# Cross-attention and routed experts on one core: x turned first in its slot, its statistics, its split and the placing of choices in other slots, a new order at the beginning

## The chip, the cores and the metric

One core of a Trainium2 chip runs the whole program. The metric is the device time of one execution in microseconds (us). The core has five engines that run in parallel, each through its own instructions in order: TensorE (PE; its weight loads are PEld), VectorE (DVE), ScalarE (ACT), GpSimd (POOL) and SyncE (SP), which here only issues transfers. They wait for one another by semaphores.

## The reference

For 64 sequences of 128 tokens with 512 features: layer norm, cross-attention to a context of 128 tokens (16 query heads on 4 heads of keys and values, head size 128, queries and keys RMS-normalised), a residual, a second layer norm, and a layer of 12 experts of which each token takes 2, with a limited number of places per expert.

```python
x = x + _L0_xattn_ref(_layernorm(x, axis=-1), ctx_2048, Wq, Wk, Wv, Wo, q_norm_w, k_norm_w)
x = x + _L0_ffn_ref(_layernorm(x, axis=-1), gate_w, w1, w2, w3)
# attention
q = rms_norm((hidden @ Wq), q_norm_w); k = rms_norm((enc @ Wk), k_norm_w); v = enc @ Wv
probs = softmax(q k^T / sqrt(128)); out = (probs @ v) @ Wo
# experts: top 2 of 12 by softmax(x @ gate_w.T), each expert takes its first cap tokens
```

## The kernel before

Two stages follow each other. The first, some 2180 us long, does attention, the second layer norm and the choice of experts; the second gathers each expert's tokens, computes and adds them. The change touches the first stage alone.

The first stage is a software pipeline. A block b is one sequence (64 of them); a slot (b, g) is one of its four steps, one for each head of keys, so g runs from 0 to 3. On each engine a function `body(b)` goes through the four slots and does in each the work of several blocks at different depths: `body` runs for b = -1 to 66, with b = 3 to 60 as a loop on the chip. What stands in `body` under `if g == ...` sets by hand the order in which each engine does things; nothing is reordered later. Semaphores only make an engine wait.

Every number is multiplied as a pair of float16: a high part, rounded on ScalarE (`split_...` of ScalarE), and the rest, formed on VectorE (`split_...` of VectorE, helpers at L1058 and L1063). A matmul takes three products of parts. Left operands must lie turned, which SyncE does by transfers (`turn_...`, L635): q, p (probabilities), k, c (context), x, xn2 (the second norm).

What the main functions are, in the order of a slot (u = 4b + g):
- TensorE: scores of u (L788), keys or values of block b+1 (L744, wkv), queries of u+3 (L744, wq; they need the turned x of block b+1 from slot (b, 1) on), the output product of u-2 (L813), attention of u-1 (L801).
- VectorE: `maxima` of the scores (L1123, L1126), low half of the outputs (L1063), other splits, `normalise` (reciprocal L1132, product L1135), low half of the probabilities (L1058, p), low half of the queries (L1114), and then one or two jobs at the end of the slot.
- ScalarE: `exps` (L943), high halves of the probabilities (L951) and queries (L933), squares of the queries (L924).
- GpSimd: roots and scales on 128 numbers or 128 x 4, and the scatter of choices to the token table (`scatter`, L1487).

The path of x, block b+2 seen from body b: loaded in slot 0 (`load_x`, L619), statistics `stats_x` (L1078, L1082) at the end of slot 0 on VectorE, reciprocal deviation `rstd_of_x` on GpSimd in slot 1, `norm_x` (L1086) at the end of slot 1, high half on ScalarE in slot 3 (L897), low half on VectorE (`split_x`, L1058) in slot 0 of body b+1, then the turn in the same slot. Choices: `choose` in slot 1 of body b+2, `count` in slot 2, `place` (L1205 to L1231) in slot 3, `scatter` in slot 0 of body b+3. `place` writes into the entries that `scatter` sends.

Before all that, the weights are scaled by their root mean square and split too. A lot is one quarter of Wq or Wo, or all of Wk or Wv (1 MB each). For each: `sum_of_lot` (squares, L1266 on VectorE or L972 on ScalarE), a total over partitions on TensorE (L736) that VectorE copies (`copy_lot_total`, L1273), the scale on GpSimd, `head_of_lot` (L979) on ScalarE and `rest_of_lot` (L1280) on VectorE. These stand between the work of the first blocks.

## Time and profile before

| | |
|---|---|
| median of 3 runs | 2544.46 us (2543.19 to 2546.59) |
| profiled execution | 2528.24 us, its span 2526.5 us |
| TensorE busy | 2277.3 us (90%) |
| VectorE busy | 1871.3 us (74%) |
| ScalarE busy | 1748.6 us (69%) |
| GpSimd busy | 1080.2 us (43%) |
| DMA moved | 348.03 MB, mean 138 GB/s |

How to read it: the busy shares are means over the run; the second stage, after some 2180 us, is less busy on all engines but GpSimd. The granted clock of TensorE is full in nearly all of the first stage. A row of a group or of a timeline gives the line, the engine, the operation, written<-read tiles, shapes and count; `[0.75 <-ACT ...]` behind it is the idle time ahead of it and what ended that. Times in a timeline are from the start of the span. Tiles are named as in the program; `work` holds probs, x_res, raw_c, raw_x and kn, and `small` all small vectors.

### The profile page before, as it was taken

Reading aid. Unit: us, or ns where it says so; the run is one execution under the profiler, and the core shown is the slowest. Engines: PE = TensorE matmul, PEld = TensorE weight load, DVE = VectorE, ACT = ScalarE, POOL = GpSimd, SP = SyncE. Lnnn points to the kernel's source line nnn. Section 1 sums busy time; section 2 is a strip of 40 time slices with the busy share of each in tenths; the row PEclk is TensorE's granted clock in tenths of the full one; section 3 lists DMA queues with packets and bytes.
Section 4 is the critical chain, followed back from the end, with each engine's and each line's share of the span. In section 5 each row is a group of like instructions: output and inputs, shape, how many; then the busy total and the mean of one; then the engine's idle time right before and its main releaser. Section 6 shows DMA issues by size and latency. Waiting matters only on the chain. (4 is left out here: it accounts for less than half of the span.)

```text
span 2526.5 us, 54978 instructions
## 1 busy us (share of the span) xinstructions
PE 2277.3 (90%) x12931; PEld 1143.1 (45%) x12931; DVE 1871.3 (74%) x5158; ACT 1748.6 (69%) x6911; POOL 1080.2 (43%) x1949
## 2 busy tenths in 40 slices
PE   3899999999999999999999999999999999659883
PEld 1444444444444444444444444444444444335541
DVE  6777777777777877777777778777777787536552
ACT  6877777777777777777767777777777777435441
POOL 6333333343343333343333333333343333268885
PEclk8999999999999999999999999999999999879775
DMA  8576666666666666666666666666666666459997
GB/s 249 101 140 131 137 133 133 130 132 133 137 131 135 141 129 132 133 133 133 133 125 141 134 136 134 134 131 135 131 138 131 137 141 130 88 151 189 174 176 96
DMA packets 894359, 348.03 MB, mean 138 GB/s; under 512 B 829004, under 2 KB 829260, under 8 KB 894288
## 3 DMA queue, kind: packets, MB, share of 16 engines
q1 hardware_dynamic: 869104, 300.20, 56.8%
q0 software_dynamic: 22912, 43.16, 9.6%
q10 hardware_dynamic: 2304, 4.24, 0.5%
q8 instruction: 14, 0.23, 0.0%
q14 instruction: 25, 0.20, 0.0%
HBM read 91.37 MB, written 57.71 MB: 59 GB/s over the span
## 5 line engine op out<-in xcount | busy, mean ns | idle before, releaser
L744 PE MATMUL pb<-wq,xT 128*128 128x512 f16 x3072 | 718.8, 384 | 93.9 <-DMA xT<-x 92.6
L943 ACT ACTIVATE work<-pb,small 128x128 f32<-128x128 f32 x1024 | 455.2, 453 | 395.2 <-DVE small L1126 395.2
L813 PE MATMUL pb<-wo,o 128*128 128x512 f16 x3072 | 711.6, 381 | 13.3 <-DVE o L1063 13.0
L1393 POOL TENSOR_TENSOR small<-small 128x4 f32<-128x4 f32 (+1 forms) x584 | 494.7, 850 | 59.8 <-POOL small L1464 18.4
L744 PEld LDWEIGHTS pb<-wq,xT 128*128 128x128 f16 x3072 | 298.5, 99 | 480.6 <-issue 137.6
L813 PEld LDWEIGHTS pb<-wo,o 128*128 128x128 f16 x3072 | 286.8, 98 | 346.4 <-DVE o L1063 17.8
L744 PE MATMUL pb<-wkv,cT 128*128 128x512 f16 x1536 | 376.6, 381 | 4.7 <-DVE wq L1280 4.7
L1464 POOL TENSOR_TENSOR small<-small 128x4 f32<-128x4 f32 x256 | 55.3, 216 | 751.7 <-ACT junk_q L924 747.2
L1114 DVE SCALAR_TENSOR_TENSOR q<-pb,small,q 128x128 f16<-128x128 f32 x1024 | 288.3, 344 | 70.4 <-ACT q L933 70.4
L933 ACT ACTIVATE q<-pb,small 128x128 f16<-128x128 f32 x1024 | 291.1, 366 | 2.6 <-POOL small L1393 1.8
L1058 DVE TENSOR_TENSOR p<-work,p 128x512 f16<-128x512 f32 x256 | 177.3, 692 | 142.9 <-ACT p L951 137.1
L924 ACT ACTIVATE junk_q<-pb 128x128 bf16<-128x128 f32 x1024 | 273.4, 305 | 5.2 <-PE pb L744 5.2
L924 ACT ACTIVATION_READ_ACCUMULATOR junk_q<-pb 128x1 f32 x1024 | 243.9, 238 | 0.0
L788 PEld LDWEIGHTS pb<-kT,qT 128*128 128x128 f16 x3072 | 193.1, 98 | 70.1 <-issue 10.2
L788 PE MATMUL pb<-kT,qT 128*128 128x128 f16 x3072 | 213.9, 219 | 8.8 <-DMA kT<-k 8.0
L951 ACT CAST p<-work 128x512 f16<-128x512 f32 x256 | 158.2, 618 | 86.0 <-DVE work L1135 85.2
L801 PE MATMUL pb<-pT,v 128*128 128x512 f16 x768 | 208.1, 380 | 0.0
L943 ACT ACTIVATION_READ_ACCUMULATOR work<-pb,small 128x1 f32 x1024 | 202.7, 198 | 0.0
L1123 DVE TENSOR_REDUCE small<-pb 128x4 f32<-128x512 f32 x256 | 176.3, 689 | 29.8 <-issue 23.1
L744 PEld LDWEIGHTS pb<-wkv,cT 128*128 128x128 f16 x1536 | 140.2, 98 | 127.8 <-DVE wq L1280 4.8
L1487 POOL DMA_INDIRECT token_table<-small x128 | 152.3, 1189 | 85.2 <-issue 68.2
L1135 DVE SCALAR_TENSOR_TENSOR work<-work,small 128x512 f32<-128x512 f32 x256 | 177.2, 692 | 8.8
(146 smaller groups left out, 2913.6 us busy)
## 6 DMA issues: line engine op xcount, KB each, us to landing
work<-x SPq DMA_DIRECT2D x128, 256.0 KB, 3.1
work<-c SPq DMA_DIRECT2D x64, 256.0 KB, 2.8
out<-work SPq DMA_DIRECT2D x64, 256.0 KB, 2.0
xn_scratch<-work SPq DMA_DIRECT2D x64, 256.0 KB, 2.1
wq_raw<-wq SPq DMA_DIRECT2D x4, 1024.0 KB, 13.3
wo_raw<-wo ACTq DMA_DIRECT2D x4, 1024.0 KB, 11.5
qT<-q SPq DMA_TRANSPOSE x256, 3.1
pT<-p SPq DMA_TRANSPOSE x256, 3.2
```

The source lines that it names most:

```text
L744: mm = nc.tensor.matmul(bank[:, :], lhs[:, NC * a + c, :], rhs[b_][:, c, :], start=(c == 0 and n == 0), stop=(c == NC - 1 and n == 2))
L788: mm = nc.tensor.matmul(S_B[:, h * 128:(h + 1) * 128], qT16[g % 2][:, 4 * a + h, :], kT16[:, 4 * b_ + g, :], start=(n == 0), stop=(n == 2))
L801: mm = nc.tensor.matmul(OT_B[:, :], v16[:, NG * a + g, :], pT16[g % 2][:, (HI, LO)[b_], :], start=(n == 0), stop=(n == 2))
L813: mm = nc.tensor.matmul(WO_B[:, :], o16[:, HPG * a + h, :], part(O0 + g, b_)[:, h, :], start=(g == 0 and h == 0 and n == 0), stop=(g == NG ...
L924: sq = nc.scalar.activation(junk_q[:, h, :], Q_BS[g % 2][:, h * 128:(h + 1) * 128], ACT.Square, scale=1.0 / QS, accum_out=q_ssq[:, h:h + 1])
L933: hi = nc.scalar.activation(q16[:, h, :], Q_BS[g % 2][:, h * 128:(h + 1) * 128], ACT.Copy, scale=q_rms[g % 2][:, h:h + 1])
L943: ex = nc.scalar.activation(probs[:, cols], S_B[:, cols], ACT.Exp, bias=nmax[:, h:h + 1], scale=esc, accum_out=psums[:, h:h + 1])
L1058: return nc.vector.tensor_tensor(pair[:, LO, :], whole.rearrange(by_head, h=4), pair[:, HI, :], ALU.subtract)
L1114: lo = nc.vector.scalar_tensor_tensor(out=q16[:, 4 + h, :], in0=Q_BS[g % 2][:, h * 128:(h + 1) * 128], scalar=q_rms[g % 2][:, h:h + 1], in ...
L1123: nc.vector.tensor_reduce(smax, heads(S_B), AX.X, ALU.max).then_inc(mx_done, 1)
L1135: nc.vector.scalar_tensor_tensor(out=pv, in0=pv, scalar=PS, in1=rsums[:, :, None].broadcast_to([128, HPG, 128]), op0=ALU.mult, op1=ALU.mul ...
L1393: return nc.gpsimd.tensor_tensor(out_, in_, neghalf[:, 0:n], ALU.pow)
```

## The change

Steady part, on each engine:
- SyncE: in slot 0, `load_x` and `turn_x` come ahead of `turn_xn2`.
- VectorE: `split_x` leaves slot 0 of the next body and becomes the last work of slot 3; `stats_x` goes from the end of slot 0 to the end of slot 1; `norm_x` from the end of slot 1 to the front of slot 3, ahead of `split_k`; `place` from the end of slot 3 to the end of the next slot 0.
- GpSimd: `scatter` from slot 0 to slot 1, `rstd_of_x` from slot 1 to slot 2.

Beginning: Wq's lots 1 to 3 are loaded by ScalarE's queue instead of SyncE's; the turn of c and the load and turn of x are issued earlier, the second c, the gate and the fill of the tables later; the sums of Wo's lots come after the work of block 0 in their slot, the loads of Wo at the end of slot (-1, 1); further sums, totals and rests change places.

```diff
@@ sync
-                for g in range(1, NG):
-                    load_lot(Q0 + g)
...
+                turn_c(0)
...
-                turn_c(0)
-                load_c(1)
-                sp.wait_ge(s_const, 1)
-                fill_tables()
...
-                        if g == 0 and live(b - 2):
-                            turn_xn2(b - 2)
                         if g == 0 and live(b + 2):
                             load_x(b + 2)
                         if g == 0 and live(b + 1):
                             turn_x(b + 1)
+                        if g == 0 and live(b - 2):
+                            turn_xn2(b - 2)
+                        if g == 0 and isinstance(b, int) and b == -1:
+                            load_c(1)
+                            sp.dma_start(gate[:, :, :], gateT).then_inc(d_gate, 16)
+                            sp.wait_ge(s_const, 1)
+                            fill_tables()
@@ scalar
                 sum_c(0)
+                load_lot(act, Q0 + 1)
                 sum_of_lot(K0)
                 split_c(0)
+                load_lot(act, Q0 + 2)
                 split_x(0)
+                load_lot(act, Q0 + 3)
                 sum_of_lot(V0)
...
-                            if g == 1:
-                                for l in ALL_O:
-                                    load_wo(l)
-                            if g == 3:
-                                sum_of_lot(O0 + 2)
-                                sum_of_lot(O0 + 3)
...
+                        if isinstance(b, int) and b == -1 and g == 1:
+                            for l in ALL_O:
+                                load_wo(l)
+                        if isinstance(b, int) and b == -1 and g == 3:
+                            sum_of_lot(O0 + 2)
+                            sum_of_lot(O0 + 3)
@@ vector
-                        if g == 0 and live(b + 1) and not (isinstance(b, int) and b == -1):
-                            split_x(b + 1)
...
+                        if g == 3 and live(b + 2):
+                            norm_x(b + 2)
                         if g == 3 and live(b + 1):
                             split_k(b + 1)
...
-                        if g == 0 and live(b + 2):
-                            stats_x(b + 2)
+                        if g == 0 and live(b - 3):
+                            place(b - 3)
                         if g == 1 and live(b - 2):
                             choose(b - 2)
                         if g == 1 and live(b + 2):
-                            norm_x(b + 2)
+                            stats_x(b + 2)
...
-                        if g == 3 and live(b - 2):
-                            place(b - 2)
+                        if g == 3 and live(b + 2):
+                            split_x(b + 2)
+                        if isinstance(b, int) and b == -1 and g == 3:
+                            sum_of_lot(O0)
+                            sum_of_lot(O0 + 1)
@@ gpsimd
-                        if g == 0 and live(b - 3):
+                        if g == 1 and live(b - 3):
                             scatter(b - 3)
-                        if g == 1 and live(b + 2):
-                            rstd_of_x(b + 2)
...
+                        if g == 2 and live(b + 2):
+                            rstd_of_x(b + 2)
```

SyncE at the start of body 2 (slot 0). Before:
```order
L635 DMA_TRANSPOSE qT_1<-q 128x8x128
L635 DMA_TRANSPOSE nT<-n 128x8x128
L619 DMA work<-x 128x512
L635 DMA_TRANSPOSE xT<-x 128x8x128
L635 DMA_TRANSPOSE pT_0<-p 128x8x128
```
The change, with its own line numbers (nine more here):
```order
L644 DMA_TRANSPOSE qT_1<-q 128x8x128
L628 DMA work<-x 128x512
L644 DMA_TRANSPOSE xT<-x 128x8x128
L644 DMA_TRANSPOSE nT<-n 128x8x128
L644 DMA_TRANSPOSE pT_0<-p 128x8x128
```
The turn of xn2 (nT) has gone behind the load and the turn of x.

VectorE from the maxima of slot (2, 3) to the end of that slot, just ahead of the loop. Before:
```order
L1123 TENSOR_REDUCE small<-pb 128x4
L1126 TENSOR_SCALAR small<-small 128x4
L1063 SCALAR_TENSOR_TENSOR o<-pb,o 128x512
L1058 TENSOR_TENSOR k<-work,k 128x512
L1132 RECIPROCAL small<-small 128x4
L1135 SCALAR_TENSOR_TENSOR work<-work,small 128x512
L1058 TENSOR_TENSOR p<-work,p 128x512
L1114 SCALAR_TENSOR_TENSOR q<-pb,small,q 128x128 x4
L1165 TENSOR_SCALAR work<-work,small 128x512
L1205 TENSOR_SCALAR small<-small 128x1
L1207 TENSOR_REDUCE small<-small 128x2
```
The change (two more in the line numbers of VectorE):
```order
L1125 TENSOR_REDUCE small<-pb 128x4
L1128 TENSOR_SCALAR small<-small 128x4
L1065 SCALAR_TENSOR_TENSOR o<-pb,o 128x512
L1088 TENSOR_SCALAR work<-work,small 128x512
L1060 TENSOR_TENSOR k<-work,k 128x512
L1134 RECIPROCAL small<-small 128x4
L1137 SCALAR_TENSOR_TENSOR work<-work,small 128x512
L1060 TENSOR_TENSOR p<-work,p 128x512
L1116 SCALAR_TENSOR_TENSOR q<-pb,small,q 128x128 x4
L1167 TENSOR_SCALAR work<-work,small 128x512
L1060 TENSOR_TENSOR x<-work,x 128x512
```
norm_x (L1086, now L1088) has come in ahead of the low half of k, and the low half of x stands where `place` began (L1205 onward, 11 operations).

VectorE from the end of slot (-1, 3) to the first maxima. Before:
```order
L1280 SCALAR_TENSOR_TENSOR wq<-wq_raw,small,wq 128x512 x4
L1266 SCALAR_TENSOR_TENSOR wo,small<-wo_raw 128x2048 x2
L1058 TENSOR_TENSOR k<-work,k 128x512
L1114 SCALAR_TENSOR_TENSOR q<-pb,small,q 128x128 x4
L1123 TENSOR_REDUCE small<-pb 128x4
```
The change:
```order
L1088 TENSOR_SCALAR work<-work,small 128x512
L1060 TENSOR_TENSOR k<-work,k 128x512
L1282 SCALAR_TENSOR_TENSOR wq<-wq_raw,small,wq 128x512 x4
L1116 SCALAR_TENSOR_TENSOR q<-pb,small,q 128x128 x4
L1060 TENSOR_TENSOR x<-work,x 128x512
L1268 SCALAR_TENSOR_TENSOR wo,small<-wo_raw 128x2048 x2
L1125 TENSOR_REDUCE small<-pb 128x4
```
The two squared sums of Wo have gone from ahead of the low half of k to behind everything else of the slot. TensorE's order is the same in both.

## Rows read from the trace of the kernel before

**Rows 1.** The page: busy time of each engine, and the query matmuls' group.
```profile
PE 2277.3 (90%) x12931; PEld 1143.1 (45%) x12931; DVE 1871.3 (74%) x5158; ACT 1748.6 (69%) x6911; POOL 1080.2 (43%) x1949
...
L744 PE MATMUL pb<-wq,xT 128*128 128x512 f16 x3072 | 718.8, 384 | 93.9 <-DMA xT<-x 92.6
```

**Rows 2.** Timeline of TensorE: the scores that open one block and the next.
```profile
999.27 0.83 PE L788 MATMUL pb<-kT,qT 128*128 128x128 f16 x12
...
1030.88 0.83 PE L788 MATMUL pb<-kT,qT 128*128 128x128 f16 x12
```

**Rows 3.** The line of the row maxima, 200 to 2140 us: count, durations, first and last.
```profile
L1123 DVE TENSOR_REDUCE small<-pb x233: 677/691/693, 203.6 to 2136.1; 128x4 f32<-128x512 f32 x117
```

**Rows 4.** Waits of VectorE, 200 to 2140 us: us in total, times, longest.
```profile
DVE small L1078 <- DMA work<-x: 47.2, 54, 3.1
...
DVE small L1123 <- PE pb L788: 2.1, 7, 0.3
```

**Rows 5.** Timeline of VectorE over one block, slots 1, 2, 3, 0.
```profile
1009.29 0.69 DVE L1123 TENSOR_REDUCE small<-pb 128x4 f32<-128x512 f32 x1
...
1016.89 0.54 DVE L1086 TENSOR_SCALAR work<-work,small 128x512 f32<-128x512 f32 x1
1017.35 0.74 DVE L1151 SCALAR_TENSOR_TENSOR work<-pb,small,work 128x512 f32<-128x512 f32 x1
...
1025.44 0.69 DVE L1123 TENSOR_REDUCE small<-pb 128x4 f32<-128x512 f32 x1
...
1028.33 0.18 DVE L1132 RECIPROCAL small<-small 128x4 f32<-128x4 f32 x1 [0.75 <-ACT work L943]
...
1032.46 0.15 DVE L1205 TENSOR_SCALAR small<-small 128x1 f32<-128x1 f32 x1
...
1034.09 0.69 DVE L1123 TENSOR_REDUCE small<-pb 128x4 f32<-128x512 f32 x1 [0.40 <-issue]
...
1036.15 0.68 DVE L1058 TENSOR_TENSOR x<-work,x 128x512 f16<-128x512 f32 x1
1036.98 0.18 DVE L1132 RECIPROCAL small<-small 128x4 f32<-128x4 f32 x1
...
1040.87 0.69 DVE L1078 BATCH_NORM_STATS2 small<-work 128x6 f32<-128x512 f32 x1
...
1041.84 0.69 DVE L1123 TENSOR_REDUCE small<-pb 128x4 f32<-128x512 f32 x1
```

**Rows 6.** Waits of all engines, whole run.
```profile
DVE small L1078 <- DMA work<-x: 55.9, 58, 6.6
```

**Rows 7.** Timeline of the same block: SyncE's queue and ScalarE.
```profile
1027.65 1.23 SPq L635 DMA_TRANSPOSE kT<-k  x1
...
1036.40 0.46 ACT L943 ACTIVATE work<-pb,small 128x128 f32<-128x128 f32 x1
...
1038.44 1.24 SPq L635 DMA_TRANSPOSE xT<-x  x1
```

**Rows 8.** Landing times: of k's turn over the run, of x's by its tile.
```profile
kT<-k SPq DMA_TRANSPOSE x64, 3.1
...
DMA to landing us min/median/max: 3.6/4.1/6.7
```

**Rows 9.** Timeline of VectorE in the beginning; the page's row on the loads of Wo.
```profile
26.48 0.16 DVE L1273 TENSOR_SCALAR small<-pb 128x1 f32<-128x1 f32 x1 [2.93 <-PE pb L736]
...
41.74 0.16 DVE L1273 TENSOR_SCALAR small<-pb 128x1 f32<-128x1 f32 x1 [3.21 <-PE pb L736]
...
51.39 2.29 DVE L1266 SCALAR_TENSOR_TENSOR wo<-wo_raw 128x2048 f16<-128x2048 f32 x1
...
55.77 1.12 DVE L1114 SCALAR_TENSOR_TENSOR q<-pb,small,q 128x128 f16<-128x128 f32 x4 [1.47 <-ACT q L933]
59.02 0.69 DVE L1123 TENSOR_REDUCE small<-pb 128x4 f32<-128x512 f32 x1 [2.13 <-PE pb L788]
...
wo_raw<-wo ACTq DMA_DIRECT2D x4, 1024.0 KB, 11.5
```

More of the change, by code:

```diff
@@ L608, in loop, with load_lot @@
                     body(b)
+            wkv_v = [w.rearrange("(c p) n -> p c n", p=128) for w in (wk, wv)]
+            wq_v = wq.rearrange("(c p) n -> p c n", p=128)
+            def load_lot(eng, l):
+                kind, n = LOTS[l]
+                src = wq_v[:, :, n * 512:(n + 1) * 512] if kind == "q" else wkv_v["kv".index(kind)]
+                eng.dma_start(raw(l), src).then_inc(d_w[l], 16)
             @block.sync
@@ L661, in turn_xn2 @@
                     turn(nT16, n16, d_nT)
-                wkv_v = [w.rearrange("(c p) n -> p c n", p=128) for w in (wk, wv)]
-                wq_v = wq.rearrange("(c p) n -> p c n", p=128)
-                def load_lot(l):
-                    kind, n = LOTS[l]
-                    src = wq_v[:, :, n * 512:(n + 1) * 512] if kind == "q" else wkv_v["kv".index(kind)]
-                    sp.dma_start(raw(l), src).then_inc(d_w[l], 16)
                 def fill_tables():
@@ L679, in _ @@
                 load_c(0)
[L680 removed]
+                load_lot(sp, K0)
                 load_x(0)
[L682 to L685 removed]
+                load_lot(sp, Q0)
+                load_lot(sp, V0)
+                turn_c(0)
                 sp.dma_start(wb[:, :], qw.broadcast_to([128, HD])).then_inc(d_small, 16)
                 sp.dma_start(wk_row[:, :], kw.broadcast_to([128, HD])).then_inc(d_small, 16)
[L688 to L692 removed]
                 def body(b):
@@ L1003, in body @@
                         last = off(b, g, -2)
-                        for l in at_slot(HEADS, b, g):
-                            head_of_lot(l)
-                        if isinstance(b, int) and b == -1:
-                            if g == 0:
-                                sum_of_lot(Q0 + 3)
-                            if g == 1:
-                                for l in ALL_O:
-                                    load_wo(l)
-                            if g == 3:
-                                sum_of_lot(O0 + 2)
-                                sum_of_lot(O0 + 3)
                         if live(last[0]):
@@ L1024, in body @@
                             split_k(b + 1)
+                        for l in at_slot(HEADS, b, g):
+                            head_of_lot(l)
+                        if isinstance(b, int) and b == -1 and g == 0:
+                            sum_of_lot(Q0 + 3)
                         if live(b):
@@ L1291, in _ @@
                 copy_total(0)
+                split_x(0)
                 sum_of_lot(Q0)
-                split_x(0)
                 copy_lot_total(Q0)
@@ L1296, in _ @@
                 copy_lot_total(V0)
+                rest_of_lot(Q0)
                 sum_of_lot(Q0 + 1)
-                rest_of_lot(Q0)
                 def body(b):
@@ L1303, in body @@
                         last = off(b, g, -2)
-                        if isinstance(b, int) and b == -1:
-                            if g == 0:
-                                copy_lot_total(Q0 + 1)
-                                sum_of_lot(Q0 + 2)
-                                rest_of_lot(V0)
-                            if g == 1:
-                                copy_lot_total(Q0 + 2)
-                                rest_of_lot(Q0 + 1)
-                                scale_weights()
-                            if g == 2:
-                                copy_lot_total(Q0 + 3)
-                                rest_of_lot(Q0 + 2)
-                            if g == 3:
-                                rest_of_lot(Q0 + 3)
-                                sum_of_lot(O0)
-                                sum_of_lot(O0 + 1)
                         if g == 0 and isinstance(b, int) and b == 1:
@@ L1335, in body @@
                             norm_k(b + 1)
+                        if g == 3 and live(b + 2):
+                            norm_x(b + 2)
                         if g == 3 and live(b + 1):
                             split_k(b + 1)
+                        if isinstance(b, int) and b == -1:
+                            if g == 0:
+                                copy_lot_total(Q0 + 1)
+                                rest_of_lot(V0)
+                                sum_of_lot(Q0 + 2)
+                            if g == 1:
+                                copy_lot_total(Q0 + 2)
+                                scale_weights()
+                                rest_of_lot(Q0 + 1)
+                            if g == 2:
+                                copy_lot_total(Q0 + 3)
+                                rest_of_lot(Q0 + 2)
+                            if g == 3:
+                                rest_of_lot(Q0 + 3)
                         if live(b):
```

4 lines of the change are left out of this document (removed).

## The prediction

> **What bounds the kernel now.** I read the page first, then the waits of each engine in a long steady stretch (200 to 2140 us), then one block instruction by instruction, and last the first 60 us.
>
> The page points at TensorE: 90% busy, VectorE 74%, and one large named stall, the query matmuls (L744) held 92.6 us by the transfer that turns x [rows 1]. If that were the bound, the change would be worth those 92.6 us. So the question is who holds whom. A block in which TensorE is hardly held takes it 1030.88 - 999.27 = 31.6 us from its first scores to the next block's [rows 2]. The row maxima on VectorE (L1123) come four times a block; over the stretch their 233 starts are (2136.1 - 203.6) / 232 = 8.33 us apart, 33.3 us a block [rows 3]. TensorE is thus ahead by 1.7 us a block and has to stop somewhere. VectorE, in the same stretch, is held by TensorE for 2.1 us in all at the maxima, and by nothing else of TensorE; it stops 47.2 us for x to arrive, 0.40 us a block at the turn of its loop [rows 4, 5], and otherwise for ScalarE's halves of the same work (exp, probabilities, queries), which ScalarE in its turn can begin only when VectorE hands them over. VectorE and ScalarE form a closed chain and set the pace. TensorE's stall on x is where its spare time shows, not what it costs.
>
> The chain in one block [rows 5]: from maxima to maxima slots 1 and 2 take 1025.44 - 1009.29 = 16.15 us, slot 3 8.65, slot 0 1041.84 - 1034.09 = 7.75, together 32.55. In this block x was not waited for; with its mean wait of 47.2 / 58 = 0.81 us the block is 33.36, against the 33.3 measured. So this account of the block is complete, and the change has to be priced on it.
>
> **The change, part by part, for the chain.**
>
> *Statistics of x out of slot 0.* stats_x comes one slot later, so x has a slot, some 8 us, more to arrive. VectorE no longer waits: 55.9 us over the run, of which the first, 6.6 us, is the very first x and stays [rows 6]. That is -49.3 us. The operation itself, 1041.84 - 1040.87 = 0.97 us, is at the open end of a slot before and after and costs the same there.
>
> *Normalising x from slot 1 to slot 3.* At the end of slot 1 nothing covers it: it takes 1017.35 - 1016.89 = 0.46 us until the next operation starts. Its new place is ahead of the reciprocal in slot 3, where VectorE idles 0.75 us for the exponentials [rows 5]. It fits with 0.29 to spare: -0.46 x 62 blocks = -28.5 us. The two first blocks are part of the beginning.
>
> *Low half of x (split_x, L1058) from slot 0 to the end of slot 3.* This one goes the wrong way. In slot 0 it stands ahead of the reciprocal and ends at 1036.83, while the last exponential, which the reciprocal needs too, ends at 1036.40 + 0.46 = 1036.86 [rows 5, 7]. It was free there and taking it away gains nothing. At the end of slot 3 nothing covers its 0.68 us: +42 us over 62 blocks (0.60 each if it overlaps its neighbours as VectorE's operations do in the middle of a slot, +37).
>
> *Choices placed (place) from slot 3 to slot 0.* Its 11 small operations take from 1032.46 until the 0.40 idle before 1034.09, 1.23 us [rows 5], uncovered before and after: 0. The scatter that follows them moves to slot 1 on GpSimd, ahead of the mean squares of k. Those are needed by VectorE only in slot 2; that cover gone, each us that they were late would cost one per block.
>
> *Turn of x first.* split_x now precedes the slot, so load and turn of x can be issued as soon as SyncE has sent the queries, and are not behind the turn of xn2. In the block shown the turn was issued at 1038.44 [rows 7]; before it stood the turn of xn2, which waited for VectorE's slot 0. I expect it about 2.5 us earlier, enough for its 4.1 us to land [rows 8] ahead of the queries in nearly all blocks. The stall at L744 goes away; but TensorE will stop elsewhere, since it still is quicker than the chain: I expect at the turned k (scores, L788) and for the low half of queries and outputs. Worth by itself: 0.
>
> *The turn of k.* normalising x also stands ahead of split_k, so k's turn is issued 0.46 us later. It was issued at 1027.65 [rows 7], and lands in 3.1 us [rows 8]: with 0.46 more, 1031.21, scores done 0.83 later [rows 2], 1032.04, some 0.1 for the hand-over. The maxima of that slot would start at 1034.09 - (1.23 - 0.68) = 1033.54. So 1.4 us of slack cover this; VectorE doesn't wait.
>
> Sum for the blocks: -49.3 - 28.5 + 42.2 = -35.6 us, 0.57 a block; new pace about 32.7 us, still above TensorE's 31.6.
>
> **The beginning.** The first maxima stand at 59.02. Ahead of them VectorE idled 2.13 us for the scores and 1.47 for a slice of queries; the scores waited for k, whose low half stood behind two squared sums of Wo at 2.29 us [rows 9]. The change puts k ahead of these sums: both waits, 3.60 us, should go. Two earlier waits, 2.93 and 3.21 us for totals of weights [rows 9], hang on the second c and on the first queries, whose transfers come earlier now that three weight slices go by ScalarE's queue; I count 2 of the 6.1. Against it split_x of block 1 is done earlier, +0.7. Together -5. The bounds: -9 if all four waits go; 0 if the loads of Wo, now issued after the first squared queries and 11.5 us on the way [rows 9], come late for the sums that then stand last, or if the two queues of weights delay the v weights, on which ScalarE waits ahead of its first split.
>
> The end has no x, and its chain of choices runs in the same order: 0.
>
> **Sum.** -35.6 - 5 = -40.6 us. The profiled execution took 2528.24 us around its span of 2526.5, 16 us less than the median of the runs, 2544.46; it should come out at 2487.6. The difference carried to the median: 2503.9, say 2504.
>
> **A rule to weigh.** The Trainium skill (Perfetto Trace Analysis, Identifying Performance Opportunities) says to optimise the engine with the highest occupancy first and to look for what ends its gaps. It warns that TensorE's busy share is no good measure of its distance from the roofline, yet by the rule as it stands TensorE is the one to relieve, and its gap is the wait for x. By it this change would be worth the whole stall, which is the first rival below. The rows on who waits for whom contradict it here.
>
> **Rivals.**
> *The stall is the cost.* If relieving TensorE let the chain follow, the 92.6 us would go, with 5 at the beginning: 2447. For it: the stall is real and comes in every block. Against it: VectorE's 2.1 us of waiting for TensorE; there is almost nothing for an earlier TensorE to speed up, unless ScalarE's waits hide some.
> *The cover in slot 3 fails.* ScalarE's split of x stands in slot 3 right behind the exponentials and ahead of the probabilities. If the normalised x comes late there, the 28.5 us aren't gained: -49.3 + 42.2 - 5 = -12, 2532. The 0.29 to spare says no, narrowly.
> *Slower: k's turn.* If it took 5.5 us instead of 3.1 once it shares the queue in another rhythm, VectorE would wait 2.4 - 1.4 = 1.0 a block: +62 - 41 = +21, 2565. It decides from about 3.1 + 1.4 + 0.66 = 5.2 us on. x's turn, the same size, needs 4.1 in the median and up to 6.7 [rows 8], so it isn't absurd; in the long stretch the scores aren't held today.
> *No change.* The reciprocal root of x on GpSimd, moved to slot 2 ahead of its other work, could come late for slot 3 and give back most of what the wait for x cost: with 0.65 us a block of it, +40 - 41, 2544. Against it: a whole slot lies between, and GpSimd is 43% busy [rows 1].
>
> **How the numbers follow.** My forecast (2490 to 2518: uncovered split_x at 0.60 or 0.69 us, the beginning -9 to 0, runs scattering by 3 us) 0.64. The full stall 0.08. Cover fails or a like partial loss 0.14. No change 0.05. Slower 0.09. Faster by more than 0.2% (5 us, about what a measurement of this kernel can tell from no change) is 0.64 + 0.08 + 0.14 = 0.86, the same 0.05, slower 0.09. The range from 2476 to 2532 leaves out the full stall, the slower case and part of no change.
>
> **What would show it.** The maxima's spacing falls from 8.33 us to about 8.18, slots 1 and 2 together from 16.15 to 16.7, slot 3 from 8.65 to 8.1, slot 0 from 8.56 (with its wait) to 8.0. The waits for x on VectorE and at L744 are gone to the first; TensorE has new waits of over 1 us a block at the scores or for low halves, and is still busy as long as before. Wrong would be: VectorE's maxima waiting for scores (then k or TensorE bounds), the reciprocal in slot 3 later than before, or maxima spaced below 8.0.

## The result

The changed kernel takes 2481.03 us (median of 4 runs, 2479.44 to 2482.33); the kernel before, on the same chip, 2543.82 us (4 runs, 2538.54 to 2546.59). The ratio is 0.9755, 95% interval 0.9738 to 0.9772: 62.8 us less. The profiled executions took 2528.24 us before and 2481.03 us after (span 2479.3), 47.2 us less. The forecast was 2504, range 2476 to 2532.

The page of the changed kernel, its busy row and three groups. These answer to [rows 1] and to the line of the maxima, now L1125:
```profile
PE 2279.2 (92%) x12931; PEld 1143.6 (46%) x12931; DVE 1877.1 (76%) x5158; ACT 1749.1 (71%) x6911; POOL 1055.1 (43%) x1949
...
L744 PE MATMUL pb<-wq,xT 128*128 128x512 f16 x3072 | 709.0, 381 | 2.1 <-DMA xT<-x 1.2
...
L788 PE MATMUL pb<-kT,qT 128*128 128x128 f16 x3072 | 214.7, 220 | 37.9 <-DMA kT<-k 36.1
...
L1125 DVE TENSOR_REDUCE small<-pb 128x4 f32<-128x512 f32 x256 | 175.7, 686 | 2.6 <-issue 0.3
```
TensorE is busy as long as before; its stall on x, 92.6 us, is 1.2 us. It stops for k instead.

Waits of VectorE in the changed kernel, 200 to 2140 us (answers to [rows 4]), complete:
```profile
DVE p L1060 <- ACT p L951: 128.8, 182, 0.8
DVE small L1134 <- ACT work L943: 89.2, 188, 1.3
DVE q L1116 <- ACT q L933: 64.5, 238, 0.8
DVE small L1134 <- issue: 35.7, 52, 0.7
```
x is waited for no more, TensorE not either: the chain of VectorE and ScalarE is still closed.

One block on VectorE in the changed kernel, slots 1, 2, 3 and the start of the next (answers to [rows 5]):
```profile
1016.66 0.16 DVE L1233 TENSOR_TENSOR small<-small 128x2 int32<-128x2 f32 x1
1016.83 0.69 DVE L1125 TENSOR_REDUCE small<-pb 128x4 f32<-128x512 f32 x1
...
1024.52 0.69 DVE L1080 BATCH_NORM_STATS2 small<-work 128x6 f32<-128x512 f32 x1
...
1026.16 0.68 DVE L1125 TENSOR_REDUCE small<-pb 128x4 f32<-128x512 f32 x1
...
1033.74 0.69 DVE L1125 TENSOR_REDUCE small<-pb 128x4 f32<-128x512 f32 x1
...
1035.21 0.54 DVE L1088 TENSOR_SCALAR work<-work,small 128x512 f32<-128x512 f32 x1
...
1036.64 0.18 DVE L1134 RECIPROCAL small<-small 128x4 f32<-128x4 f32 x1 [0.29 <-ACT work L943]
...
1040.76 0.69 DVE L1060 TENSOR_TENSOR x<-work,x 128x512 f16<-128x512 f32 x1
1041.37 0.68 DVE L1125 TENSOR_REDUCE small<-pb 128x4 f32<-128x512 f32 x1
```
The normalising of x (L1088) stands in the gap ahead of slot 3's reciprocal and leaves 0.29 of its 0.75 us. The low half of x (L1060) stands uncovered at the slot's end, 0.61 us. The maxima behind it begin at once: the 0.40 us of idle time at the loop's turn [rows 5] is gone, which was not foreseen. The last of the eleven operations of the placing (L1233) now stands directly ahead of the maxima of slot 1, with no turn of the loop between them, and no idle time is seen there.

The beginning on VectorE in the changed kernel (answers to [rows 9]):
```profile
56.76 1.13 DVE L1116 SCALAR_TENSOR_TENSOR q<-pb,small,q 128x128 f16<-128x128 f32 x4 [5.36 <-ACT q L933]
...
58.40 2.28 DVE L1268 SCALAR_TENSOR_TENSOR wo<-wo_raw 128x2048 f16<-128x2048 f32 x1
...
60.61 2.29 DVE L1268 SCALAR_TENSOR_TENSOR wo<-wo_raw 128x2048 f16<-128x2048 f32 x1
...
62.82 0.69 DVE L1125 TENSOR_REDUCE small<-pb 128x4 f32<-128x512 f32 x1
```
The wait for queries is 5.36 us instead of 1.47, and both squared sums of Wo now stand between it and the first maxima. The scores that these maxima read, on TensorE, in the kernel before:
```profile
57.54 1.44 PE L788 MATMUL pb<-kT,qT 128*128 128x128 f16 x12 [8.02 <-DMA kT<-k]
```
And in the changed kernel:
```profile
57.42 1.44 PE L788 MATMUL pb<-kT,qT 128*128 128x128 f16 x12 [6.90 <-DMA kT<-k]
```
The scores end as early as before, 57.42 + 1.44 = 58.86 instead of 58.98. The maxima follow them at once before (59.02), and 3.96 us later in the changed kernel (62.82), when VectorE has done the sums.

Where the 47.2 us of the profiled executions lie: first maxima at 62.82 instead of 59.02, +3.8; from the first to the last of the 256 maxima 2067.7 instead of 2124.2, -56.5; behind them 348.8 instead of 343.3, +5.5.

### The profile page after: what moved, and what is told of

It reads as the page before. It is cut to its first block and busy times, and to the rows that moved or that the text cites. A ratio compares the mean times of both kernels' runs of the same rounds, so it can differ in the third digit from the quotient of the medians.

```text
span 2479.3 us, 54980 instructions
## 1 busy us (share of the span) xinstructions
PE 2279.2 (92%) x12931; PEld 1143.6 (46%) x12931; DVE 1877.1 (76%) x5158; ACT 1749.1 (71%) x6911; POOL 1055.1 (43%) x1949
## 5 line engine op out<-in xcount | busy, mean ns | idle before, releaser
L744 PE MATMUL pb<-wq,xT 128*128 128x512 f16 x3072 | 709.0, 381 | 2.1 <-DMA xT<-x 1.2
L1396 POOL TENSOR_TENSOR small<-small 128x4 f32<-128x4 f32 (+1 forms) x584 | 484.1, 833 | 60.9 <-POOL small L1467 18.4
L744 PEld LDWEIGHTS pb<-wq,xT 128*128 128x128 f16 x3072 | 300.8, 98 | 367.3 <-DVE q L1116 13.6
L744 PE MATMUL pb<-wkv,cT 128*128 128x512 f16 x1536 | 377.1, 382 | 2.9 <-DVE wkv L1282 2.9
L1060 DVE TENSOR_TENSOR p<-work,p 128x512 f16<-128x512 f32 x256 | 177.3, 692 | 142.9 <-ACT p L951 137.1
L788 PE MATMUL pb<-kT,qT 128*128 128x128 f16 x3072 | 214.7, 220 | 37.9 <-DMA kT<-k 36.1
L744 PEld LDWEIGHTS pb<-wkv,cT 128*128 128x128 f16 x1536 | 140.3, 98 | 126.1 <-issue 3.3
L1125 DVE TENSOR_REDUCE small<-pb 128x4 f32<-128x512 f32 x256 | 175.7, 686 | 2.6 <-issue 0.3
L1065 DVE SCALAR_TENSOR_TENSOR o<-pb,o 128x512 f16<-128x512 f32 x256 | 175.0, 683 | 2.6 <-ACT o L957 2.5
```

What stands on the lines that cost most here:

```text
L744: mm = nc.tensor.matmul(bank[:, :], lhs[:, NC * a + c, :], rhs[b_][:, c, :], start=(c == 0 and n == 0), stop=(c == NC - 1 and n == 2))
L788: mm = nc.tensor.matmul(S_B[:, h * 128:(h + 1) * 128], qT16[g % 2][:, 4 * a + h, :], kT16[:, 4 * b_ + g, :], start=(n == 0), stop=(n == 2))
L1060: return nc.vector.tensor_tensor(pair[:, LO, :], whole.rearrange(by_head, h=4), pair[:, HI, :], ALU.subtract)
L1125: nc.vector.tensor_reduce(smax, heads(S_B), AX.X, ALU.max).then_inc(mx_done, 1)
L1396: return nc.gpsimd.tensor_tensor(out_, in_, neghalf[:, 0:n], ALU.pow)
```

## What each kernel's slots take

From the starts of the maxima on VectorE, mean of the 51 blocks between the 25th and the 229th of them, in us. Times are medians; "before" is the kernel before on the chip of the same runs. The slots of each kernel are from its one trace, that of "before" too. The runs below went in three sets, each on one chip: e1 to e4, f0 to f3, f4 to f7.

| kernel | slot 0 | slot 1 | slot 2 | slot 3 | block | time | before | ratio, 95% |
|---|---|---|---|---|---|---|---|---|
| before | 8.54 | 8.73 | 7.48 | 8.65 | 33.41 | | | |
| changed | 7.87 | 9.33 | 7.58 | 7.63 | 32.41 | 2481.0 | 2543.8 | 0.9755 (0.9738 to 0.9772) |
| e1_norm2_last | 9.31 | 8.76 | 7.53 | 8.29 | 33.89 | 2558.1 | 2524.4 | 1.0132 (1.0106 to 1.0158) |
| e2_stats_alone | 6.79 | 9.46 | 7.54 | 8.65 | 32.45 | 2475.2 | 2524.4 | 0.9804 (0.9779 to 0.9830) |
| e3_old_queue_order | 7.87 | 9.34 | 7.58 | 7.63 | 32.42 | 2474.5 | 2524.4 | 0.9797 (0.9772 to 0.9821) |
| e4_split_x_covered | 7.87 | 9.34 | 7.58 | 7.02 | 31.81 | 2439.3 | 2524.4 | 0.9661 (0.9637 to 0.9686) |
| f0_changed_again | 7.87 | 9.33 | 7.58 | 7.63 | 32.41 | 2480.3 | 2557.0 | 0.9700 (0.9683 to 0.9717) |
| f1_lots_late | 7.87 | 9.33 | 7.58 | 7.63 | 32.40 | 2482.8 | 2557.0 | 0.9707 (0.9691 to 0.9724) |
| f2_wo_early | 7.87 | 9.33 | 7.58 | 7.63 | 32.40 | 2478.4 | 2557.0 | 0.9697 (0.9681 to 0.9713) |
| f3_best | 7.87 | 9.33 | 7.57 | 7.02 | 31.79 | 2446.7 | 2557.0 | 0.9573 (0.9557 to 0.9589) |
| f4_place_alone | 8.84 | 8.73 | 7.43 | 7.02 | 32.01 | 2454.6 | 2543.6 | 0.9643 (0.9619 to 0.9667) |
| f5_place_last | 6.64 | 9.33 | 7.46 | 9.24 | 32.68 | 2498.3 | 2543.6 | 0.9816 (0.9793 to 0.9839) |
| f6_wo_early_covered | 7.86 | 9.33 | 7.57 | 7.02 | 31.78 | 2441.9 | 2543.6 | 0.9593 (0.9570 to 0.9616) |
| f7_gaps | 7.87 | 8.52 | 7.27 | 7.78 | 31.45 | 2420.7 | 2543.6 | 0.9510 (0.9482 to 0.9538) |

## The experiments on the blocks

**e1_norm2_last.** VectorE's slot 3 of the kernel before in another order: the placing no longer last.
```diff
-                        if g == 3 and live(b - 1):
-                            norm2(b - 1)
                         if g == 3 and live(b - 2):
                             place(b - 2)
+                        if g == 3 and live(b - 1):
+                            norm2(b - 1)
```


> The kernel before with one swap: in slot 3 VectorE places the choices first and then does the second norm (one operation of 0.54 us), so a long operation and not eleven short ones stands ahead of the turn of its loop. Theory A (the 0.40 us idle ahead of the maxima of slot 0 is time in which VectorE's instruction stream turns the loop, seen because the short operations don't cover it): the idle goes, slot 3 falls from 8.65 to about 8.25, 58 blocks, -23 us against before. Theory B (the idle is the price of the loop's turn whatever stands ahead): no change, and the 0.48 us by which slot 3 fell more than I priced came from elsewhere.

Measured: 2558.1 us, 34 slower than before. Both theories missed the time; slot 3 did as A said. It fell from 8.65 to 8.29 us, and the idle time at the loop's turn is gone. But slot 0 grew by 0.77. VectorE's wait for x, 200 to 2100 us:
```profile
DVE small L1078 <- DMA work<-x: 89.1, 57, 3.6
```
And one slot 0 in the timeline, with SyncE's queue:
```profile
1008.95 0.69 DVE L1123 TENSOR_REDUCE small<-pb 128x4 f32<-128x512 f32 x1
...
1011.47 1.23 SPq L635 DMA_TRANSPOSE nT<-n  x1
...
1012.95 0.41 SPq L619 DMA_DIRECT2D work<-x  x1
...
1016.76 0.69 DVE L1078 BATCH_NORM_STATS2 small<-work 128x6 f32<-128x512 f32 x1 [1.08 <-DMA work<-x]
```
The load is issued 4.00 us behind the slot's maxima; in the block of [rows 5] it was 3.69. The queue's own waits, 200 to 2100 us, say why:
```profile
SPq L434 <- DVE work L1165: 97.0, 56, 1.7
```
In the kernel before this wait is 32.8 us. It is that of the store of the second normalisation's result (L632, `store_xn2`), which stands in the queue ahead of the turn of queries, of the turn of xn2 (nT) and of the load of x. The low half of xn2 itself is not later: it starts 1.47 us behind the maxima in both kernels. The wait for x rose from 47.2 us [rows 4] to 89.1, 0.7 us a block; besides the 0.3 us of later issue, the load also took longer to land, 4.1 us in the median against 3.7. So that wait lies on a loop from VectorE over SyncE's queue back to VectorE, and a small delay of an operation that feeds the queue cost more than the order saved.

**e2_stats_alone.** The kernel before with the statistics of x in slot 1, the root in slot 2 and the normalising in slot 3; the low half of x and the placing stay where they were.
```diff
-                        if g == 0 and live(b + 2):
-                            stats_x(b + 2)
...
                         if g == 1 and live(b + 2):
-                            norm_x(b + 2)
+                            stats_x(b + 2)
...
+                        if g == 3 and live(b + 2):
+                            norm_x(b + 2)
```


> The kernel before with only the statistics of x moved to slot 1, its reciprocal deviation to slot 2 on GpSimd and its normalising to slot 3; the low half of x stays in slot 0, choices stay in slot 3, the queue's order and the beginning stay. Theory A (VectorE and ScalarE are a closed chain that sets the pace): the wait for x goes (-49) and the normalising is covered (-28), together about -75 us against before, more than the whole change gave, while TensorE still waits for the turned x in some blocks. Theory B (TensorE's wait for the turned x is the cost): the turned x comes no earlier in its slot, so little is won, 0 to -20 us.

Measured: -49 us, between the two, in the blocks -0.96 us. The wait for x is gone. What kept it from A's size shows in all engines' waits, 200 to 2100 us:
```profile
ACT o L957 <- PE pb L801: 117.2, 127, 2.3
...
PE pb L744 <- DMA xT<-x: 44.2, 48, 2.7
...
DVE small L1123 <- PE pb L788: 9.9, 41, 0.6
```
Here the chain is no longer closed: TensorE still waits 44.2 us for the turned x, ScalarE waits for TensorE's outputs (117.2 us, before 20.3), VectorE for its scores. That the turn of x stands where it was is not enough to explain it: in f4 and e3 it stands there too, and TensorE's wait for it is 1.4 and 0.8 us. What e2 has otherwise than these two is the write of the choices (`scatter`, GpSimd) still in slot 0, and a slot 0 shorter by 1 to 2 us; which of them counts, no run separates. The idle time at the loop's turn is as before, 22.3 us, since the placing still stands last.

**f4_place_alone.** The kernel before with the placing moved, and with it, of need, the write of the choices on GpSimd one slot later.
```diff
+                        if g == 0 and live(b - 3):
+                            place(b - 3)
                         if g == 0 and live(b + 2):
                             stats_x(b + 2)
...
-                        if g == 3 and live(b - 2):
-                            place(b - 2)
...
-                        if g == 0 and live(b - 3):
+                        if g == 1 and live(b - 3):
                             scatter(b - 3)
```


> The kernel before with one part of the change alone: the eleven small operations of the choices' placing go from the end of slot 3 to slot 0 ahead of the statistics of x (and the write of their table one slot later on GpSimd). Theory A (this part alone removes both the wait for x, 0.8 us a block, since it stands under it, and the 0.40 us in which VectorE stands at its loop's turn behind these operations): slot 3 falls from 8.65 to about 7.0 us, slot 0 rises from 8.5 to about 9.0, together -1.2 us a block, -75 us. Theory B (the idle time at the loop's turn has nothing to do with them): -0.8 us a block, -50 us. Theory C (x is late whatever stands ahead of it, because its load is due later too): -20 us or less.

Measured: 2454.6 against 2543.6, -89 us: more than the whole change gives. Theory A holds for the slots (7.02 and 8.84 for 7.0 and 9.0); its -75 us was 14 too little. Its timeline of all engines:
```profile
1024.86 0.68 DVE L1123 TENSOR_REDUCE small<-pb 128x4 f32<-128x512 f32 x1
...
1028.97 0.38 SPq L619 DMA_DIRECT2D work<-x  x1
...
1032.74 0.69 DVE L1078 BATCH_NORM_STATS2 small<-work 128x6 f32<-128x512 f32 x1
```
The load in the block of [rows 5], from the timeline of the kernel before:
```profile
1037.78 0.38 SPq L619 DMA_DIRECT2D work<-x  x1
```
There it is issued 3.69 us behind the slot's maxima, in f4 4.11, so no earlier. But the statistics are wanted 7.88 us behind the maxima instead of 1040.87 - 1034.09 = 6.78. The eleven small operations are a cover of 1.10 us, of which the later issue takes 0.42.

They are not the whole of it, since the load also lands sooner. The load of x from issue to landing, 200 to 2100 us, in the kernel before:
```profile
DMA to landing us min/median/max: 2.9/3.7/6.2
```
And in f4:
```profile
DMA to landing us min/median/max: 2.7/2.9/3.1
```
An estimate from these figures: with f4's landings even the kernel before would hardly wait, since its load would be there at the latest 3.69 + 3.1 = 6.79 us behind the maxima, for statistics wanted at 6.78. With the landings of before, f4 would still wait in some blocks: 4.11 + 6.2 = 10.3 at the most, for 7.88. What else moved in f4 is the write of the choices. In the kernel before it stands just ahead of the load (issued at 1037.78):
```profile
1034.97 1.12 POOL L1487 DMA_INDIRECT token_table<-small  x1 [0.76 <-issue]
...
1036.40 1.29 POOL L1487 DMA_INDIRECT token_table<-small  x1 [0.31 <-issue]
```
In all three kernels with this write in slot 0 (before, e1, e2) the load lands in 3.6 to 4.1 us in the median and up to 6.3; in those with it a slot later, in 2.9 us or less. So the write is a rival of the cover: f4 does not tell which of the two took the wait away, and no run moves the write by itself.

**f5_place_last.** The changed kernel with the placing at the end of slot 3 again, behind the low half of x.
```diff
-                        if g == 0 and live(b - 3):
-                            place(b - 3)
...
                         if g == 3 and live(b + 2):
                             split_x(b + 2)
+                        if g == 3 and live(b - 2):
+                            place(b - 2)
```


> The changed kernel with the placing last in slot 3 again, behind the split of x. Theory A (the loop's turn costs 0.40 us a block when eleven operations of 0.15 us stand ahead of it and nothing behind one of 0.5 us or more): slot 0 falls by 1.2 and slot 3 rises by 1.2 + 0.4 us, the period goes from 32.41 to 32.8 us, +26 us: 2506. Theory B (the idle went with something else, the load of the loop's own instructions for example): the period stays at 32.4 and the time at 2480.

Measured: 2498.3, where A had 2506 and B 2480; the block 32.68 instead of 32.8. A's mechanism came, its size in part. VectorE at its loop's turn:
```profile
1014.58 0.15 DVE L1231 TENSOR_SCALAR small<-small 128x1 f32<-128x1 f32 x1
1014.70 0.16 DVE L1233 TENSOR_TENSOR small<-small 128x2 int32<-128x2 f32 x1
1015.26 0.69 DVE L1125 TENSOR_REDUCE small<-pb 128x4 f32<-128x512 f32 x1 [0.40 <-issue]
```
And that wait, 200 to 2100 us:
```profile
DVE small L1125 <- issue: 22.3, 56, 0.4
```
The 0.40 us is back in every one of 56 blocks: slots 0 and 3 take 15.89 us instead of 7.87 + 7.63 = 15.50. The rest is slot 2, 0.12 shorter; why, no run tells.

**e4_split_x_covered.** The changed kernel with the low half of x back in slot 0, ahead of the reciprocal.
```diff
                         if g == 0 and live(b - 2):
                             split_xn2(b - 2)
+                        if g == 0 and live(b + 1) and not (isinstance(b, int) and b == -1):
+                            split_x(b + 1)
...
-                        if g == 3 and live(b + 2):
-                            split_x(b + 2)
```


> The changed kernel with the low half of x back in slot 0, ahead of the reciprocal, where VectorE idles 0.75 us for the exponentials in the changed kernel. Theory A (closed chain; this move was the change's loss): 0.60 us a block less, -37 us against the changed kernel, 2444; if the 0.40 us at the turn of the loop come back, since the operation that now stands last is the shorter second norm, 2467. Theory B (the turned x must come early): the turn goes behind slot 0's work again and TensorE is held by it, 2481 or slower.

Measured: 2439.3, and 35 us below e3 beside it; slot 3 fell by 0.61 and no other slot changed. So this move of the change cost what it was priced at, 0.60 us a block, and bought nothing. The idle time at the loop's turn does not return with the second normalisation (0.54 us) last.

**e3_old_queue_order.** The changed kernel with SyncE's turn of xn2 ahead of the load and the turn of x, as before.
```diff
+                        if g == 0 and live(b - 2):
+                            turn_xn2(b - 2)
                         if g == 0 and live(b + 2):
                             load_x(b + 2)
                         if g == 0 and live(b + 1):
                             turn_x(b + 1)
-                        if g == 0 and live(b - 2):
-                            turn_xn2(b - 2)
```


> The changed kernel with SyncE's old order alone: in slot 0 the turn of xn2 stands ahead of the load and the turn of x again. Theory A (closed chain on VectorE and ScalarE): the time of the changed kernel within 3 us, 2478 to 2484. Theory B (the early turn of x is what gains): x is turned some 1.5 us later and a part of the stall of before returns, 2500 or more.

Measured: 2474.5, below A's 2478 to 2484, and the same slots to 0.01 us. The turn of x first is worth nothing, as A said. TensorE's wait for the turned x, 200 to 2100 us:
```profile
PE pb L744 <- DMA xT<-x: 0.8, 2, 0.5
```
The stall of the kernel before (88.1 us in this stretch) stays away with the turn in its old place, issued 4.33 us behind the maxima in the mean, in before 4.35. So it was not the earlier turn that ended it.

## The experiments on the beginning

**f0_changed_again** is the changed kernel, unedited.

> The changed kernel unedited, on the chip of the runs beside it, as the level for them. Theory A (the time of before hangs on when x lands, that of the changed kernel does not): before moves with the chip, the changed kernel stays at 2474 to 2484 us. Theory B (chips differ alike for both): the ratio to before is 0.9755 again whatever the chip.

Measured: 2480.3, where before took 2557.0. The ratio is 0.9700 instead of 0.9755, their intervals apart, so theory B is out and A's numbers hold. Over four sets of runs before stood at 2524.4, 2543.6, 2543.8 and 2557.0; the changed kernel, in two of them, at 2481.0 and 2480.3, and e3, with the same slots, at 2474.5 beside the 2524.4. That it is the landing of x that makes before differ is argued; only one execution of it has a trace.

**f1_lots_late.** The changed kernel with ScalarE's loads of Wq behind its sum of v's weights.
```diff
                 sum_c(0)
-                load_lot(act, Q0 + 1)
...
                 sum_of_lot(V0)
+                load_lot(act, Q0 + 1)
+                load_lot(act, Q0 + 2)
+                load_lot(act, Q0 + 3)
```


> Beginning only: the changed kernel with ScalarE's three loads of lots of Wq (1, 2, 3) issued behind its sum of v's weights. Theory A (v's weights landed 4.2 us later, at 17.5 instead of 13.2 us, because the load of Wq's lot 1 runs beside theirs): the sum of v's weights starts at about 13.3 us, the first maxima at 59 to 60 instead of 62.8 us, and the time falls by 2 to 4 us. Theory B (something else holds the beginning, above all the landing of k and q turned for the first block): the sum is earlier and the first maxima stay at 62.5 to 63 us. The blocks stay at 32.41 us each.

Measured: 2482.8, not told from f0 by the time; the first maxima at 65.2 us, 2 later than in f0. The sum of v's weights did come early, as A said, and the Wq lots then came too late. The sum of v's weights on ScalarE, in the timeline of the kernel before:
```profile
13.23 1.91 ACT L972 ACTIVATE wkv<-wkv_raw 128x2048 f16<-128x2048 f32 x1 [2.34 <-DMA wkv_raw<-wv]
```
The same in the changed kernel:
```profile
17.47 1.91 ACT L972 ACTIVATE wkv<-wkv_raw 128x2048 f16<-128x2048 f32 x1 [6.43 <-DMA wkv_raw<-wv]
```
The same in f1, and VectorE's copy of a total there:
```profile
12.95 1.91 ACT L972 ACTIVATE wkv<-wkv_raw 128x2048 f16<-128x2048 f32 x1 [2.15 <-DMA wkv_raw<-wv]
...
32.27 0.16 DVE L1275 TENSOR_SCALAR small<-pb 128x1 f32<-128x1 f32 x1 [8.37 <-PE pb L736]
```
The sum came 4.5 us earlier, and the wait for the total of the next lot took 8.37 us, in the changed kernel 1.51.

**f2_wo_early.** The changed kernel with ScalarE's loads of Wo at the start of slot 1 of block -1.
```diff
+                        if isinstance(b, int) and b == -1 and g == 1:
+                            for l in ALL_O:
+                                load_wo(l)
                         if live(last[0]):
                             split_o(*last)
```


> Beginning only: the changed kernel with ScalarE's loads of Wo issued at the start of slot 1 of block -1 again, as before the change. Theory A (the turns of q and k before the first scores are late because 4 MB of Wo, issued at 39.9 to 42.2 us, run beside them): the loads are issued some 6 us earlier, the waits of 4.6 us for q's landing and 6.9 us for k's shrink by 4 to 5 us together with the first maxima, from 62.8 to about 58 us, and the time falls by 4 to 5 us. Theory B (the turns are late by their own chain: root and split of k): no change, first maxima at 62.5 to 63 us. The blocks stay at 32.41 us each.

Measured: 2478.4, the first maxima at 60.54 us against 63.26 in f0: -2.7. By the time alone that is not told from no change (interval of the ratio to before 0.9681 to 0.9713, f0's 0.9683 to 0.9717); the trace shows the mechanism. SyncE's queue in the changed kernel:
```profile
47.71 1.38 SPq L644 DMA_TRANSPOSE qT<-q  x1
49.20 4.37 SPq L644 DMA_TRANSPOSE cT<-c  x1
53.66 1.71 SPq L644 DMA_TRANSPOSE kT<-k  x1
```
And in f2:
```profile
48.99 1.27 SPq L644 DMA_TRANSPOSE cT<-c  x1
50.35 1.29 SPq L644 DMA_TRANSPOSE kT<-k  x1
```
In the changed kernel the turn of c holds the queue 4.37 us instead of 1.27, and k's turn goes 3.3 us later. Two of the four loads of Wo were then still under way (they landed at 51.27 and 54.83); in f2 all had landed by 46.49. A's size, 4 to 5 us, was too large by half.

## Versions made from the runs

**f3_best** is e4 with the edits of f1 and f2.

> A version made from what the runs showed: the changed kernel with the split of x back in slot 0 under the exponentials (which took 0.60 us a block off), ScalarE's Wq loads behind its sum of v's weights and its Wo loads early. Theory A (the blocks and the beginning add up): blocks of 31.81 us, 2430 to 2440 us. Theory B (the beginning is covered by something else, or a block falls into TensorE's floor of 31.5 us and waits return): 2439 us or more.

Measured: 2446.7, 33.6 below f0. The blocks are A's 31.79; the first maxima, at 62.75, gained almost nothing (f1's loss and f2's gain are about as large). Theory B's time.

**f6_wo_early_covered** is e4 with f2's edit alone.

> A version made from what the runs showed: the changed kernel with the split of x back in slot 0 under the exponentials, and ScalarE's Wo loads early; the Wq loads stay where the change put them. Theory A (both gains add up): first maxima at about 60 us, blocks of 31.80 us, 2435 to 2438 us. Theory B (a block of the covered version gains nothing from an earlier beginning): 2440 to 2447.

Measured: 2441.9. The first maxima (60.18) and the blocks (31.78) are A's, the time is B's: in its profiled execution what lies behind the last maxima took 353.0 us, against 339 to 349 in most others. That part was not looked into.

**f7_gaps** is f6 with three operations moved into the gap between the normalise and the split of P.
```diff
                         if g == 0 and live(b + 2):
                             split_c(b + 2)
+                        if g == 1 and live(b + 2):
+                            stats_x(b + 2)
+                        if g == 2 and live(b - 1):
+                            stats_2(b - 1)
+                        if g == 3 and live(b - 1):
+                            norm2(b - 1)
                         if live(b):
                             split_p(*cur)
...
-                        if g == 1 and live(b + 2):
-                            stats_x(b + 2)
-                        if g == 2 and live(b - 1):
-                            stats_2(b - 1)
-                        if g == 3 and live(b - 1):
-                            norm2(b - 1)
```


> The version beside it with three more operations under cover: the statistics of x in slot 1, those of the second normalisation in slot 2 and that normalisation in slot 3 stand between the normalise and the split of P, where VectorE waits 0.7 us for ScalarE. Theory A (the pace now passes to TensorE, which was busy 1880 of 1900 us in the covered version): blocks of 31.5 us, -20 us, 2416. Theory B (the chain through VectorE and ScalarE still sets it, and each operation delays the split of P by more than it saves): no gain or up to 20 us slower.

Measured: 2420.7, 21 below f6 and the fastest of all: 0.9510 of before. Theory A holds in the blocks, 5 us short in the time. One of VectorE's waits, 200 to 2100 us:
```profile
DVE small L1125 <- PE pb L788: 103.8, 113, 1.1
```
VectorE now waits for scores, 103.8 us where it was 2.1 [rows 4]: the chain has come down to TensorE, whose block takes 31.45 us.

## Why the prediction was right, and where it was off

The sign, the range and the reason hold: VectorE and ScalarE set the pace, TensorE's stall on x was a symptom. That stall went, 92.6 to 1.2 us, for a gain of half its size (47.2 us between the profiled executions). The rival by which it was the whole cost (2447) is out. By the rule of the Trainium skill (Perfetto Trace Analysis, Identifying Performance Opportunities), to start at the engine of highest occupancy, this stall was the thing to remove. The runs disagree: in e3 the stall is 0.8 us, and e4, beside it, is 35 us faster by one operation of 0.69 us moved on VectorE. f4 by itself would not decide, since its 89 us come with the stall gone too.

The point that VectorE was free of TensorE holds only where the turned x comes in time; e2 shows a version in which it doesn't.

Term by term, for the profiled executions (predicted -40.6, measured -47.2):

- *Wait for x, -49.3.* It is gone, as priced: slot 0 was to fall to 8.0 and is 7.87. But the statistics' move was named as the cause, and in f4 the wait goes with the statistics where they were. Each of the two changes is enough, and the gain is not to be had twice. The write of the choices moved from beside the load, which the prediction looked at for GpSimd alone, may have a part: the load lands in 2.9 us instead of 3.7 without it (f4).
- *Normalising x under cover, -28.5.* The 0.29 us left in the gap are the very ones predicted.
- *Low half of x uncovered, +42.2.* 0.61 us a block in e4, some 38: the prediction's other value (0.60) was the right one, the sum took 0.68.
- *Placing, 0.* This step failed. It was priced by its own 1.23 us, the same in both places; the 0.40 us behind it at the loop's turn were seen, and subtracted from its length, but taken for a property of the loop. They belong to what stands last in it: e1, e4, f4 and f5 agree. -0.40 us at each of 58 turns is -23 us. The blocks gave 21 us beyond their sum (-56.5 against -35.6): these 23, 4 of the low half of x, some 8 in slot 0 (7.87 for 8.0), less 11 in slots 1 and 2, together 24.
- *Slots 1 and 2, 16.7.* 16.91: 0.1 more in slot 1 and 0.1 in slot 2 than the operations moved would give, both unexplained.
- *Turn of x first and k's turn, 0.* Right, and TensorE's new waits are at the scores, as expected, 37.9 us in all. But the earlier turn was named as what ends the stall at L744, and e3 and f4 have the turn in its old place with 0.8 and 1.4 us of stall. The turned x lands in 3.5 us in both and in 4.1 in the kernel before (medians); which of the other moves ended the stall stays open.
- *Beginning, -5.* Wrong sign, +3.8. The gain was eaten ahead of the first scores, which end at 58.86 instead of 58.98: Wq's lot 1 made v's weights 4.2 us later (17.47 instead of 13.23), which was named as a bound, and the loads of Wo delayed the turns. The loss itself is the two sums of Wo behind the scores, 3.96 us. The prediction asked whether their loads would be late for them; they were not (no idle time ahead of 58.40). What it left out is that the sums now stand between the scores and the maxima.
- *The end, 0.* +5.5 between two single executions; the others spread from 339 to 353 us, so it is no effect shown.
- *From the profiled execution to the median, +16.3.* This was the largest miss on the forecast: 16 of its 23 us. The changed kernel's profiled execution equals its median. That fits a chain in which x's landing no longer stands: before varied by 33 us over four sets, the changed kernel (with e3) by 7 over three. No run shows it directly, since only one execution of before has a trace.

In the blocks the change is a sum of three: 33.41 to 32.01 by the placing and the write of the choices (f4), to 31.81 by statistics and normalising of x (e4), back up to 32.41 by the low half of x.

## To carry to other kernels

Find the closed chain by asking which engine never waits for the busiest one, and price each moved operation by what is uncovered in its new place; ask too what lands while it runs, since small operations can be the cover of a transfer, and what other transfers a moved operation starts, beside whose load they then run. Read idle time "for nothing" at a loop's turn as belonging to the instructions ahead of it, and try the order of the last ones. Where a chain holds a transfer's landing, its profiled execution may be lucky (argued here, not shown): don't carry the difference to the median over to a kernel that has taken the landing out.

## What the runs showed of the hardware

At the turn of VectorE's loop 0.40 us are lost when eleven operations of 0.15 us stand ahead of it (22.3 us in 56 blocks, in before, e2 and f5), and nothing when one of 0.54 us or more does (changed, e1, e3, e4, f4). The same eleven ahead of maxima without a turn lose nothing (changed, 1016.66 to 1016.83). The Trainium skill (Perfetto Trace Analysis, DVE / Act Engine Instruction) describes a sequencer that decodes ahead of the engine into a wait queue and an execution queue. By that account a run of short operations would empty them before the turn's own instructions are through; the runs agree, but none shows a queue's filling.

A turn by transfer (that of c) held SyncE's queue 4.37 us instead of 1.27 while loads of 1 MB from another engine's queue were under way. Not every turn did: that of q, issued 1.5 us ahead of it beside the same loads, held it 1.38 us.

A load of 256 KB beside GpSimd's indirect writes landed later than the same load away from them, in both places where the runs put it. The load of x in slot 0 took 3.6 to 4.1 us in the median, up to 6.3, with the writes in slot 0 (before, e1, e2) and 2.9 us with them in slot 1 (e3, f4). The second load of x, in slot 1, took 2.7 us with the writes in slot 0 (before, e1, e2), and with them in slot 1 up to 4.5 us in e3 and 4.3 in the median, up to 5.9, in e4. Other moves differ between these kernels too, so the writes are the likely cause and not a shown one.
